# A three-layer decoder, one core: the row transposes issued ahead of the weight share's loads, and the share's thresholds and comparison moved on VectorE

## The chip, the core and the metric

The kernel runs on one core of one Trainium2 chip. The time is the device time of one execution, in microseconds (us). Before the change three runs gave 1193.79, 1201.42 and 1203.77 us, median 1201.42. The five engines each work through their own list of instructions in order, and wait for each other on semaphores: TensorE (PE) multiplies matrices, VectorE (DVE) and ScalarE (ACT) work element by element, GpSimd (POOL) does so more slowly, and SyncE (SP) issues the transfers (DMA).

## What is computed

The input `x` has 8 batches of 256 tokens and 512 features. Three residual layers follow one another:

```python
x = x + _L0_attn_ref(_layernorm(x), Wq, Wk, Wv, Wo, bo)          # 32 query heads, 8 key groups of 64, causal, tanh cap
x = x + _L0_xattn_ref(ctx_2048, ctx_2048, _layernorm(x), ssm_kernel, D, 8)
x = x + _L0_ffn_ref(_layernorm(x), w_gate_up, w_proj)
```

The feed-forward layer first rounds its weights to three values per group of 64, and this rounding is done on the chip as well:

```python
w = w_fp32.astype(bfloat16); w_g = w.reshape(-1, 64)
scale = clip(mean(abs(w_g)), 1e-8, None)
w_hat = clip(round(w_g / scale), -1, 1) * scale          # a gate_up matrix of 4096 x 512, a projection of 512 x 2048
return w + (w_hat - w)
```

## The kernel before

**Stages.** The attention of the eight batches comes first (up to about 645 us), then the convolution layer, then the feed-forward layer. Only the attention stage is touched.

**One batch of attention.** PE runs ten steps (`attend`, `STEPS = NG + 2`). In step s it does one piece of projection or output work (`filler`), the scores of head group s (`scores`), and the weighted values of group s - 2 (`values`). ACT applies tanh and exp (`soften`), POOL masks (`mask`, line 1989) and adds key halves (`add_keys`, line 1998), and DVE normalises (`normalise`). The normalised context of a group, in `ctx32`, is split in two halves of 16 bits: ACT writes the high one (`high_ctx`, line 1153), POOL the low one (`low_ctx`, line 2002), and PE's `output(b, g)` needs both.

**The tail of a batch.** Behind the ten steps PE alternates the first seven projection units of the next batch with the last three output groups: `project(b+1, 0)`, `output(b, 5)`, `project(b+1, 1)`, `output(b, 6)`, `project(b+1, 2)`, `output(b, 7)`, and then `project(b+1, 3)` to `project(b+1, 6)`. DVE turns each unit by the rotary angles (`rotate`, lines 1443 to 1446), POOL adds its parts, ACT and DVE split it (`high_unit`, `low_unit`), and SP stores it and places it again in the layout of the scores.

**The rows' turn.** The next batch's rows, standardised, are split by ACT (line 1192) and DVE (line 1625) in step 7 into `row_halves`. `turn_rows` on SP sends them through two transposing transfers into `hT_halves` (line 605). The first matmul of `project(b+1, 0)` waits for both.

**The weight share.** In each of seven batches one share of the feed-forward weights is quantised. It has 3584 columns on 128 partitions. For share b:
- SP stores the ternary weights of share b - 1 (`store_ffn`), waits until these have left, and issues the two loads of share b into `wffn` (`next_share`, lines 478 and 468, 1280 and 512 KB);
- ACT rounds them to bfloat16 in step 8 (`round_share`, line 1163), between `high_ctx(b, 5)` and `high_ctx(b, 6)`;
- DVE takes the sums and thresholds in step 9 (`find_thresholds`, lines 1562 to 1570), ahead of `normalise(b, 7)`;
- ACT spreads the thresholds over the columns into `w_cut` (`spread`, line 1167), ahead of `high_ctx(b, 7)`, and the scales behind units 1 and 2;
- DVE compares above in the tail ahead of unit 1 (`find_above`, line 1574), below in step 0 of the next batch (`find_below`, lines 1579 to 1583), and then scales the digits (`scale_digits`).

`w_cut` lies in the score buffer that group 2 uses, so ACT waits at step 2 of the next batch until `find_below` is through. SP's order around the end of a batch is `store_x2`, `late_units`, `store_ffn`, `next_share`, and in `next_inputs`: the residual's load (line 465), `turn_rows`, the load of x (line 462), and the stores and placements of the next batch's units.

## Time and profile before

| | before |
|---|---|
| runs | 1193.79, 1201.42, 1203.77 us, median 1201.42 |
| the profiled execution | 1197.75 us, its span 1196.0 us |
| PE busy | 1140.1 us (95%) |
| PE weight loads | 814.4 us (68%) |
| DVE busy | 885.7 us (74%) |
| ACT busy | 552.2 us (46%) |
| POOL busy | 679.4 us (57%) |
| mean granted clock of PE | 0.984 of full speed |

PE is busy nearly all the time, so the idle stretches of PE and the stretches in which it runs at a lower granted clock are what a change of order can win or lose. The chain that ended last is PE for the most part. A group of instructions is read as: line, engine, operation, output and inputs, and how often. Of the timeline's rows the first number is the start in us from the span's beginning, the second the duration, and brackets at the end hold the idle time ahead of the instruction and what ended it. "x2" means that the row merges two instructions.

### The profile page before, as it was taken

How to read it: one execution, taken by the hardware profiler on the slowest of the kernel's cores; microseconds unless marked ns; L12 is line 12 of the kernel's file. 1: busy time of each engine (PE TensorE's matmuls, PEld its weight loads, DVE VectorE, ACT ScalarE, POOL GpSimd, SP SyncE). 2: the span in 40 equal slices, each digit the busy share in tenths (PEclk: the TensorE clock that was granted, in tenths of full speed). 3: DMA queues.
4: the chain of work that ended last, by engine and by line, in shares of the span. 5: the costliest groups of instructions: out<-in, count | busy, mean ns of one | idle time of the engine just before them, and what ended most of it. 6: DMA issues, size and time to landing. Idle time of an engine off the chain costs nothing. (4 is left out here: it accounts for less than half of the span.)

```text
span 1196.0 us, 27031 instructions
## 1 busy us (share of the span) xinstructions
PE 1140.1 (95%) x10867; PEld 814.4 (68%) x10882; DVE 885.7 (74%) x1287; ACT 552.2 (46%) x617; POOL 679.4 (57%) x557
## 2 busy tenths in 40 slices
PE   5988998999999989999999999999999999999998
PEld 4665665756657657666576577777886876786683
DVE  6979787787788878888888588888746645754654
ACT  6866574564655645746556500000244533542441
POOL 1553492783865945947659679999343322422331
PEclk9998998998999999999999999999999999999999
DMA  9562344563454345445545457773001122013000
GB/s 325 157 227 79 120 122 119 154 170 93 150 173 141 125 120 172 141 126 155 159 140 161 170 109 142 141 142 92 1 19 23 32 54 53 8 45 53 19 19 36
DMA packets 166183, 134.15 MB, mean 112 GB/s; under 512 B 69628, under 2 KB 127362, under 8 KB 166082
## 3 DMA queue, kind: packets, MB, share of 16 engines
q1 hardware_dynamic: 141128, 126.44, 36.8%
q10 hardware_dynamic: 24960, 6.29, 3.5%
q8 instruction: 78, 1.28, 0.4%
q14 instruction: 17, 0.14, 0.0%
HBM read 81.76 MB, written 35.21 MB: 98 GB/s over the span
## 5 line engine op out<-in xcount | busy, mean ns | idle before, releaser
L701 PE MATMUL bank<-hT_halves,w_hi 128*128 128x256 f16 x640 | 179.5, 280 | 25.9 <-DMA hT_halves<-parts 20.6
L702 PE MATMUL bank<-hT_halves,w_hi 128*128 128x256 f16 x640 | 179.0, 280 | 0.0
L703 PE MATMUL bank<-hT_halves,w_lo 128*128 128x256 f16 x640 | 178.9, 280 | 0.0
L1984 POOL TENSOR_TENSOR parts<-parts 128x512 f32<-128x512 f32 x80 | 116.8, 1463 | 107.6 <-DVE parts L1446 107.6
L963 PE MATMUL bank<-kv,toep 128*128 128x288 f32 (+2 forms) x660 | 159.3, 404 | 0.7 <-ACT qT L1211 0.5
L2002 POOL TENSOR_TENSOR ctx_lo<-ctx,ctx_hi 128x512 f16<-128x512 f32 x64 | 97.7, 1526 | 89.6 <-ACT ctx_hi L1153 88.6
L963 PEld LDWEIGHTS bank<-kv,toep 128*128 128x128 f32 x660 | 124.6, 191 | 34.4 <-ACT qT L1211 0.8
L1989 POOL TENSOR_SCALAR_AFFINE_SELECT region_c<-region_c 128x512 f32<-128x512 f32 x128 | 105.5, 847 | 52.9 <-ACT region_c L1177 52.9
L2132 POOL TENSOR_TENSOR sqsum<-sqsum,toep 128x512 f32<-128x512 f32 x56 | 78.1, 1395 | 95.3 <-ACT toep L1353 95.1
L1159 ACT CAST halves<-parts 128x512 f16<-128x512 f32 x80 | 49.3, 617 | 141.4 <-POOL parts L1984 140.2
L1042 PE MATMUL bank<-odd_halves,guT 128*128 128x256 f16 x512 | 112.2, 273 | 0.0
L1041 PE MATMUL bank<-odd_halves,guT 128*128 128x256 f16 x512 | 112.2, 273 | 0.0
L1598 DVE TENSOR_TENSOR halves<-parts,halves 128x512 f16<-128x512 f32 x80 | 75.6, 944 | 49.3 <-ACT halves L1159 48.8
L1041 PE MATMUL bank<-cpair,guT 128*128 128x256 f16 x496 | 108.8, 273 | 0.3 <-DVE hid L1863 0.3
L1042 PE MATMUL bank<-cpair,guT 128*128 128x256 f16 x496 | 108.8, 273 | 0.0
L1174 ACT ACTIVATE region_c<-bank,cap_scale 128x1536 f32<-128x1536 f32 x64 | 98.1, 1532 | 20.7 <-PE bank L782 20.7
L1365 ACT ACTIVATE silu<-bank 128x512 f32<-128x512 f32 x64 | 38.0, 594 | 141.9 <-PE bank L1042 138.5
L701 PE MATMUL bank<-region_o,ctx_hi 128*128 128x512 f16 x256 | 98.3, 384 | 0.3 <-DVE parts L1446 0.2
L702 PE MATMUL bank<-region_o,ctx_hi 128*128 128x512 f16 x256 | 97.8, 382 | 0.0
L703 PE MATMUL bank<-region_o,ctx_lo 128*128 128x512 f16 x256 | 97.5, 381 | 0.0
L1177 ACT ACTIVATE region_c<-region_c 128x1536 f32<-128x1536 f32 x64 | 95.0, 1485 | 2.0
L701 PEld LDWEIGHTS bank<-hT_halves,w_hi 128*128 128x128 f16 x640 | 64.2, 100 | 44.6 <-issue 29.9
(192 smaller groups left out, 2663.2 us busy)
## 6 DMA issues: line engine op xcount, KB each, us to landing
unit_halves<-halves SPq DMA_DIRECT2D x80, 256.0 KB, 2.2
q_both<-unit_halves SPq DMA_DIRECT2D x64, 256.0 KB, 2.9
q_high<-unit_halves SPq DMA_DIRECT2D x64, 128.0 KB, 3.0
toep<-kernel_padded SPq DMA_DIRECT2D x32, 256.0 KB, 3.9
wffn<-w_gu SPq DMA_DIRECT2D x6, 1280.0 KB, 6.3
cpair<-ctx_pairs SPq DMA_DIRECT2D x32, 176.0 KB, 4.6
xin<-x SPq DMA_DIRECT2D x8, 512.0 KB, 3.9
region_o<-wq SPq DMA_DIRECT2D x4, 1024.0 KB, 11.4
```

The source lines that it names most:

```text
L701: pe.matmul(dst, lh, rh, start=first and k == 0, stop=False)
L702: pe.matmul(dst, lh, rl, start=False, stop=False)
L703: mm = pe.matmul(dst, ll, rh, start=False, stop=last and k == n - 1)
L963: mm = pe.matmul(dst, toep[:, n, d * P:(d + 1) * P], kv[:, p, m * B + batches.start:m * B + batches.stop, :], start=(m == 0), stop=(m == l))
L1041: pe.matmul(dst, guT[:, k, col:col + P], h3_hi[p][:, k, :], start=(k == 0), stop=False)
L1042: mm = pe.matmul(dst, guT[:, k, col:col + P], h3_lo[p][:, k, :], start=False, stop=(k == DB - 1))
L1174: act.activation(s.rearrange("p (n c) -> p n c", n=3), bank[:, 0:3, :], ACT.Tanh, scale=cap_scale[:, g // 2:g // 2 + 1]).then_inc(tanh_don ...
L1177: act.activation(s, s, ACT.Exp, scale=CAP).then_inc(exp_done, 1)
L1984: pool.tensor_tensor(slot[:, 0], slot[:, 0], slot[:, 1], ALU.add).then_inc(unit_summed, 1)
L1989: last = pool.affine_select(s, s, pattern=[[0, REP], [sign, P]], compare_op=ALU.is_ge, fill=0.0, base=0, channel_multiplier=-sign)
L2002: pool.tensor_tensor(ctx_lo[:, 2 * g:2 * g + 2, :], ctx32[:, g % 2], ctx_hi[:, 2 * g:2 * g + 2, :], ALU.subtract).then_inc(ctx_lo_done, 1)
L2132: pool.tensor_tensor(sqsum[:, p], sqsum[:, p], square[:, n % 2], ALU.add).then_inc(sqsum_done, 1)
```

## The change

Three things move, and no instruction is added or removed.

1. On SP, `turn_rows(b + 1)` goes from behind `next_share(b)` and `next_residual` to the place right behind `store_ffn(b - 1)`. The share's two loads and the residual's load follow it. This holds for all six batches that have a share's load at their end.
2. On DVE, `find_thresholds(b)` goes from step 9, ahead of `normalise(b, 7)`, to the tail, behind `rotate(b+1, 0)`. On ACT the spreads of the thresholds go behind units 1 and 2, and those of the scales behind units 3 and 4.
3. On DVE, `find_above` goes from the tail to step 0 of the next batch, ahead of `find_below`. The share of batch 0 has only this third part on DVE.

```diff
             def next_inputs(b):
+                turn_rows(b + 1)
+                next_share(b)
                 next_residual(b, 4 * TT * b + 2 * TT)
-                turn_rows(b + 1)
                 load_x(b + 2)
                 place_early(b + 1)
...
                 store_ffn(b - 1)
-                next_share(b)
                 next_inputs(b)
...
                 act.wait_ge(sums_filled, NG * b + LAST_IN_CUT + 1)
-                for tiles in HALVES:
-                    spread(b, gthr, w_cut, THRESHOLDS, tiles)
                 high_ctx(b, NG - 1, False)
                 for n in range(EARLY):
                     high_unit(b + 1, n)
                     if 1 <= n < 3:
-                        spread(b, gscale, w_by, THRESHOLDS, HALVES[n - 1])
+                        spread(b, gthr, w_cut, THRESHOLDS, HALVES[n - 1])
+                    if 3 <= n < 5:
+                        spread(b, gscale, w_by, THRESHOLDS, HALVES[n - 3])
...
             def attend(b):
                 for step in range(STEPS):
                     if step == 0:
+                        find_above(b - 1)
                         find_below(b - 1)
...
-                    if step == NG + 1:
-                        find_thresholds(b)
...
                 for n in range(EARLY):
-                    if n == 1:
-                        find_above(b)
                     rotate(b + 1, n)
+                    if n == 0:
+                        find_thresholds(b)
```

On SP, at the end of batch 1 (the copy ahead of the loop; the loop's copy and the last one move in the same way), the order stands as follows. `hT_halves<-parts` is the rows' turn, `wffn<-w_gu` and `wffn<-w_p` are the share's loads, `xres<-x` the residual's, `xin<-x` that of the batch after.

```order
 L487 DMA gate_up_ternary<-wffn 128x2x512
 L482 DMA proj_ternary<-wffn 128x2x256 x4
+L605 DMA_TRANSPOSE hT_halves<-parts 128x8x128 x2
 L478 DMA wffn<-w_gu 128x5x512
 L468 DMA wffn<-w_p 128x4x256
 L465 DMA xres<-x 128x2x512
-L605 DMA_TRANSPOSE hT_halves<-parts 128x8x128 x2
 L462 DMA xin<-x 128x2x512
 L527 DMA unit_halves<-halves 128x4x256 x2
```

The two transposes have moved past three loads.

On DVE, from step 9 of a batch on, before the change: the thresholds (lines 1562 to 1570), and behind them the normalisation of group 7 (lines 1455 to 1466).

```order
L1562 TENSOR_REDUCE gthr<-w_bf 128x56
L1564 ISA
L1565 TENSOR_SCALAR gscale<-gthr 128x56
L1566 REGISTER_ALU
L1567 TENSOR_SCALAR gthr<-gscale 128x56
L1568 REGISTER_ALU
L1570 TENSOR_SCALAR gthr<-gthr 128x56
L1454 REGISTER_ALU
L1455 STREAM_TRANSPOSE region_c<-bank 128x256
L1457 RECIPROCAL rinv<-region_c 128x8
L1459 STREAM_TRANSPOSE region_c<-rinv 128x256
L1466 TENSOR_TENSOR ctx<-bank,region_c 128x512
```

After the change the normalisation of group 7 stands ahead of this piece, which begins with the rotation of unit 0. Lines of the changed kernel are one lower than those of before here.

```order
L1439 ISA
L1442 TENSOR_TENSOR parts<-bank,cos_s 128x512
L1444 SCALAR_TENSOR_TENSOR parts<-bank,sin_s 128x256
L1445 TENSOR_TENSOR parts<-bank,sin_s 128x256
L1561 TENSOR_REDUCE gthr<-w_bf 128x56
L1563 ISA
L1564 TENSOR_SCALAR gscale<-gthr 128x56
L1565 REGISTER_ALU
L1566 TENSOR_SCALAR gthr<-gscale 128x56
L1567 REGISTER_ALU
L1569 TENSOR_SCALAR gthr<-gthr 128x56
```

The thresholds have moved behind one normalisation and one rotation.

On DVE, the start of the loop's body (step 0 of a batch), before the change:

```order
L1765 ISA
L1579 TENSOR_TENSOR region_c<-w_bf,region_c 128x3584
L1580 REGISTER_ALU
L1581 TENSOR_SCALAR region_c<-region_c 128x3584
L1582 REGISTER_ALU
L1583 TENSOR_TENSOR wffn<-wffn,region_c 128x3584
```

and after it, with the comparison above in front (line 1573, which was 1574):

```order
L1763 ISA
L1573 TENSOR_TENSOR wffn<-w_bf,region_c 128x3584
L1577 ISA
L1578 TENSOR_TENSOR region_c<-w_bf,region_c 128x3584
L1579 REGISTER_ALU
L1580 TENSOR_SCALAR region_c<-region_c 128x3584
L1581 REGISTER_ALU
L1582 TENSOR_TENSOR wffn<-wffn,region_c 128x3584
```

Step 0 on DVE holds one instruction over 3584 columns more.

## Rows read from the trace of the kernel before

**Rows 1.** Waits of PE: line, releaser, us in total, times, longest us.

```profile
PE bank L701 <- DMA hT_halves<-parts: 20.6, 6, 5.0
```

**Rows 2.** Timeline of PE: first matmul of project(b+1, 0), batches 1 to 4.

```profile
187.67 0.37 PE L701 MATMUL bank<-hT_halves,w_hi 128*128 128x256 f16 x1 [5.00 <-DMA hT_halves<-parts]
...
271.12 0.37 PE L701 MATMUL bank<-hT_halves,w_hi 128*128 128x256 f16 x1 [4.50 <-DMA hT_halves<-parts]
...
352.53 0.27 PE L701 MATMUL bank<-hT_halves,w_hi 128*128 128x256 f16 x1 [2.08 <-DMA hT_halves<-parts]
...
433.76 0.27 PE L701 MATMUL bank<-hT_halves,w_hi 128*128 128x256 f16 x1 [5.03 <-DMA hT_halves<-parts]
```

**Rows 3.** Timeline of SP: turns and share loads at the ends of batches 1 to 4.

```profile
179.66 4.50 SPq L605 DMA_TRANSPOSE hT_halves<-parts  x2
...
263.60 5.44 SPq L605 DMA_TRANSPOSE hT_halves<-parts  x2
...
341.55 0.39 SPq L478 DMA_DIRECT2D wffn<-w_gu  x1
...
347.43 2.97 SPq L605 DMA_TRANSPOSE hT_halves<-parts  x2
350.61 0.43 SPq L462 DMA_DIRECT2D xin<-x  x1
...
421.31 0.40 SPq L478 DMA_DIRECT2D wffn<-w_gu  x1
...
425.55 6.13 SPq L605 DMA_TRANSPOSE hT_halves<-parts  x2
```

**Rows 4.** Timeline of PE: first matmul of output(b, 6), batches 1 to 4.

```profile
197.46 0.38 PE L701 MATMUL bank<-region_o,ctx_hi 128*128 128x512 f16 x1
...
281.83 0.38 PE L701 MATMUL bank<-region_o,ctx_hi 128*128 128x512 f16 x1
...
360.35 0.38 PE L701 MATMUL bank<-region_o,ctx_hi 128*128 128x512 f16 x1
...
443.25 0.38 PE L701 MATMUL bank<-region_o,ctx_hi 128*128 128x512 f16 x1
```

**Rows 5.** Busy us (and instructions) of PE, PEld, DVE, ACT, POOL; PEclk, DMA, GB/s.

```profile
271.60:275.60 4.00, 4.00 (x21) 2.82 (x20) 3.90 (x5) 0.00 (x0) 1.16 (x1) 0.50 0.17 65
```

**Rows 6.** Timelines of ACT, POOL and DVE behind the share's load, batches 3 and 4.

```profile
349.28 3.18 ACT L1163 CAST w_bf<-wffn 128x3584 bf16<-128x3584 f32 x1 [2.45 <-DMA wffn<-w_p]
352.37 0.62 ACT L1153 ACTIVATE ctx_hi<-ctx 128x512 f16<-128x512 f32 x1
...
353.07 1.15 POOL L2002 TENSOR_TENSOR ctx_lo<-ctx,ctx_hi 128x512 f16<-128x512 f32 x1 [4.72 <-ACT ctx_hi L1153]
...
352.49 3.89 DVE L1562 TENSOR_REDUCE gthr<-w_bf 128x56 f32<-128x3584 bf16 x1 [1.80 <-ACT w_bf L1163]
...
430.50 3.18 ACT L1163 CAST w_bf<-wffn 128x3584 bf16<-128x3584 f32 x1 [5.55 <-DMA wffn<-w_p]
```

**Rows 7.** The page's DMA issues: count, KB each, median us to landing.

```profile
wffn<-w_gu SPq DMA_DIRECT2D x6, 1280.0 KB, 6.3
```

**Rows 8.** Timelines of DVE, POOL and PE: batch 2's tail, batch 3's steps 0 to 2.

```profile
278.98 2.03 DVE L1574 TENSOR_TENSOR wffn<-w_bf,region_c 128x3584 bf16<-128x3584 bf16 x1 [0.28 <-ACT region_c L1167]
...
279.56 2.46 POOL L2002 TENSOR_TENSOR ctx_lo<-ctx,ctx_hi 128x512 f16<-128x512 f32 x1 [6.75 <-ACT ctx_hi L1153]
...
304.76 2.02 DVE L1579 TENSOR_TENSOR region_c<-w_bf,region_c 128x3584 bf16<-128x3584 bf16 x1
...
307.94 2.33 DVE L1583 TENSOR_TENSOR wffn<-wffn,region_c 128x3584 bf16<-128x3584 bf16 x1
...
307.25 3.53 POOL L1989 TENSOR_SCALAR_AFFINE_SELECT region_c<-region_c 128x512 f32<-128x512 f32 x2 [3.85 <-ACT region_c L1177]
310.86 1.28 POOL L1998 TENSOR_TENSOR key_sum<-region_c 128x512 f32<-128x512 f32 x1
...
312.73 0.43 PE L814 MATMUL bank<-region_c,sum_ones 128*32 128x128 f32 x8
```

More of the change, by code:

```diff
@@ L616, in _ @@
             store_first_ffn()
-            next_share(1)
             next_inputs(1)
@@ L627, in _ @@
             store_ffn(B - 3)
+            turn_rows(B - 1)
             next_share(B - 2)
             next_residual(B - 2, 4 * TT * (B - 2) + 2 * TT)
-            turn_rows(B - 1)
             place_early(B - 1)
@@ L1655, in last_batch @@
                     if step == 0:
+                        find_above(b - 1)
                         find_below(b - 1)
@@ L1761, in first_batch @@
                 low_unit(1, EARLY - 1)
-                find_above(0)
             first_batch()
```

## The prediction, made before the changed kernel ran

> **What bounds the kernel now.** I read the page first: PE is busy 95% of the span, so what counts is where PE stands still or is slow. The list of PE's waits names one wait that comes back: the first matmul of `project(b+1, 0)` waits for the rows' turn six times, 20.6 us together [rows 1]. The timeline of PE shows four of the six: 5.00, 4.50, 2.08 and 5.03 us [rows 2]. The other two must share 20.6 - 16.61 = 3.99 us, so they are short ones like that of batch 3. So there are three long and three short waits.
>
> SP's timeline says why they differ. I call T the start of the first transpose's issue, the point at which the row halves are ready; the change leaves it alone. In batch 3 the share's load had been issued 5.9 us ahead of T (341.55 to 347.43), the two transposes took 2.97 us to issue, and PE began at T + 5.1. In batches 1, 2 and 4 they took 4.50, 5.44 and 6.13 us, and PE began at T + 8.0, 7.5 and 8.2 [rows 2, 3]; in batch 4 the load had started only 4.2 us before. The long waits are turns that queue behind a load still in flight.
>
> The long ones cost more than the wait. From `project(b+1, 0)` to `output(b, 6)` lie one output group and two projection units. That takes 7.82 us in batch 3, but 9.79, 10.71 and 9.49 us in batches 1, 2 and 4 [rows 2, 4]. Behind the idle stretch PE runs at a granted clock of 0.50, which is the 1.2 GHz level, where it had the full 2.4 GHz before [rows 5]. After the 2.08 us of batch 3 nothing of this is left over. So a long wait costs some 1.7 to 2.9 us on top.
>
> **Part 1, the turns ahead of the loads.** It gives every turn the conditions of batch 3 or better: PE can begin at T + 5.1 and reach `output(b, 6)` at T + 5.1 + 7.82 = T + 12.9. If this were all, it would be worth the sum of the offsets of `output(b, 6)` from T. These are 17.80, 18.23, 12.92 and 17.70 us now [rows 3, 4], and 12.92 for the other two: 92.5 us, against 77.5 us. That is a gain of 15.0 us.
>
> But the loads now queue behind the turns, and somebody waits for them: ACT's `round_share` stands ahead of `high_ctx(b, 6)`, and `output(b, 6)` needs that group's context. Step by step:
> - The load of x, which stood next behind the turns, was issued at T + 3.18 (347.43 to 350.61). The share's first load takes that place, after a wait for stores which left before T.
> - From its issue to ACT's start on the share took 7.73 us in batch 3 (341.55 to 349.28), giving T + 10.9.
> - The cast holds ACT for 3.09 us before `high_ctx` starts, POOL's `low_ctx` starts 0.70 us later and takes 1.15 us [rows 6]. That gives T + 15.9.
>
> PE arrives at T + 12.9 and waits 3.0 us. Before the change the load came 9 us earlier against T, and this chain was done by 354.22, 6.1 us ahead of PE's 360.35. The move uses up that cover and 3.0 us more. Six ends at T + 15.9 are 95.4 us against 92.5: **+2.9 us**. The three long ends win about 2 us each, the three short ones lose 3 us each. All later work of the tail hangs on this start, since PE runs from there to the next batch without a gap.
>
> The bounds: the longest way from load to cast is that of batch 4, 9.19 us (421.31 to 430.50), though a turn ran beside it; that adds 1.46 us to each end, 8.8 us. The shortest that a row allows is the larger load alone, 6.3 us [rows 7], which takes off 1.43 us each, 8.6 us. I take batch 3's 7.73, since there the load had the DMA engines nearly to itself, as it will behind the turns.
>
> **Part 2, the thresholds in the tail.** `find_thresholds` waits for the cast, which ends at T + 14.1. Ahead of `normalise(b, 7)` it would now hold that back too; behind `rotate(b+1, 0)` it holds back `rotate(b+1, 1)`. Its reduce takes 3.89 us [rows 6] and three short instructions follow, so it ends near T + 18.7 and the rotation near T + 20. PE needs that rotation first at `project(b+1, 4)`. At 2.6 us for each piece this begins four pieces behind `output(b, 6)`, at T + 26. The cover is 6 us, and the cost nothing. The spreads move on ACT with 2 us or more between the units. `output(b, 7)` is not late: its normalisation no longer waits. Cost: nothing.
>
> **Part 3, the comparison above in step 0.** It is one instruction of 2.03 us [rows 8]. On DVE it is covered: the rotation of unit 7 comes at most 2.03 us later, and POOL, busy masking, adds that unit's parts only well behind the first two masks. ACT's wait for `find_below` at step 2 would end at 312.3 instead of 310.3 (307.94 + 2.33), which delays the tanh of group 2 by under a microsecond; PE needs that one only behind its next projection.
>
> POOL is another matter. While DVE compares, POOL's `low_ctx` takes 2.46 us, where alone it takes 1.15 [rows 6, 8]. In step 0 POOL must mask group 0 and add its key halves for PE's sums. Before: `find_below` holds DVE from 304.76 to 310.27, the mask (two selects) takes 3.53 us, the key addition ends at 312.14, and PE takes it at 312.73, with 0.6 us to spare [rows 8]. After: with 2.03 us in front, the three instructions run to about 312.3. The mask waits for the first of them (to 308.8) and can end near 310.1, beside the second. The key addition then meets the third (310.0 to 312.3) and ends near 313.6. PE waits 0.9 us. The loop has this six times (batches 1 to 6): 6 x 0.9 = **+5.4 us**. Bounds: nothing, if POOL slips in between the instructions; or 6 x 2.1 = 12.6 us, if the mask itself waits until 312.3, ends its second select at 312.9 and the values start 1.5 us late with the key addition behind them at 314.2. The batch after the loop scales in step 1, where PE already waits for the key addition; I count nothing there.
>
> **The sum.** The profiled execution took 1197.75 us (span 1196.0). 1197.75 + 2.9 + 5.4 = **1206 us**. The median of the runs shown is 1201.42, 3.7 us more than this execution. The number of long waits is a matter of a microsecond between load and turn, so other executions will have had more of them; the change makes all ends alike, which is why I do not add the 3.7.
>
> **Rivals.**
> - **The clock falls in the new gap.** The 3.0 us ahead of `output(b, 6)` lie between 2.08 us, behind which nothing is lost, and 4.50 us, behind which 2.9 us are lost [rows 2, 4]. If it falls each time at the mean of the three losses (1.97, 2.89, 1.67: 2.2 us), that is 13 us: 1219 us; at half of the ends, 1213. Against it: 3.0 is nearer to the short wait. Chance 0.17.
> - **The load arrives early enough: faster.** This decides from one point: ACT's start on the share, 7.73 us behind the issue. If it fell to 6.3 us, the whole would be 1197.5, about no change; for the full gain it must be 4.7 us, and then 1197.75 - 15.0 + 5.4 = 1188 us. For it: the long turns really vanish. Against it: the larger of the two loads alone needs 6.3 us [rows 7]. With the POOL wait absent as well it is 1183. Chance 0.12.
> - **POOL's mask waits for all of DVE's step 0:** 1197.75 + 2.9 + 12.6 = 1213 us. For it: the mask took 3.53 us, of which about 2.3 are one DVE instruction. Against it: one of its selects ran beside the middle DVE instruction, which the change leaves in its place. Chance 0.08.
> - **The load is as slow as in batch 4:** 1206 + 8.8 = 1215 us. Chance 0.08.
>
> The Trainium skill, page "SBUF — State Buffer", section "Who interferes with whom", bears on the third rival. By it a VectorE instruction with two SBUF inputs, and a tensor_scalar in a two-port mode, hold the port pair that GpSimd reads through for the whole instruction, and the second to issue fully blocks. The trace agrees in the 2.46 us of `low_ctx`. By this rule alone the mask would also stand still beside the middle instruction, which gives the 1213 us; the 3.53 us say that one select got through, and I follow the row.
>
> **How the numbers follow.** The forecast (ends at T + 15.9, POOL between nothing and 0.9 us) has 0.55 and the range 1198 to 1212. With the rivals the range that leaves out 2 in 10 is 1190 to 1217. A measurement of this kernel tells about 1% (12 us) from no change. Faster by that is only most of the second rival: 0.10. Slower (above 1213.4): most of the clock's case, half of the last two, and a tail of the forecast: 0.20. Within 1%: 0.70.
>
> **What the profile after would show.** The waits for the rows' turn fall to six of about 2 us, 12 us together. A new wait of PE appears for POOL's `low_ctx` ahead of `output(b, 6)`, six of about 3 us, 18 us together. ACT, free near T, stands still for the share's load until T + 10.9. PE's wait for `key_sum`, 0.5 us now, grows to about 5 us. SP's transposes take 3.0 us in pairs everywhere. I am wrong if ACT starts on the share before T + 9, if PE shows no wait for the context, or if the granted clock falls behind the new gap.

## Result, and the profile after

The changed kernel takes 1226.16 us (median of four runs, 1221.73 to 1230.32), where the kernel before takes 1197.61 beside it. The ratio is 1.0263, with a 95% interval of 1.0218 to 1.0308: it is slower by 28.6 us. The forecast was 1206 us with a range up to 1217, so the time lies outside.

| | before | after |
|---|---|---|
| the profiled execution | 1197.75 us, span 1196.0 | 1230.32 us, span 1228.6 |
| PE busy | 1140.1 us (95%) | 1148.3 us (93%) |
| DVE busy | 885.7 us | 879.9 us |
| POOL busy | 679.4 us | 684.9 us |
| mean granted clock of PE | 0.984 | 0.982 |

The list of PE's waits of the kernel after, in the four lines that the change touches (line and releaser, us in total, times, longest):

```profile
PE bank L700 <- POOL ctx_lo L2000: 26.5, 6, 4.8
...
PE bank L700 <- DMA hT_halves<-parts: 8.6, 6, 1.5
PE bank L813 <- POOL key_sum L1996: 5.1, 6, 1.0
...
PE bank L700 <- DVE parts L1445: 4.6, 6, 1.6
```

The line of the rows' turn answers to [rows 1]: 20.6 us of waiting have become 8.6. The context's wait was not there before, and the other two stood at 0.5 and 0.2 us:

```profile
PE bank L814 <- POOL key_sum L1998: 0.5, 1, 0.5
PE bank L701 <- DVE parts L1446: 0.2, 1, 0.2
```

The three lines now hold 36.2 us, and the turn gives back 12.0. PE is also busy 8.2 us longer, though its work is the same.

One end of a batch shows how it goes. Here are SP, ACT, POOL and PE at the end of batch 2, where T is 268.51 (start, duration, instruction, idle time ahead of it):

```profile
268.51 2.79 SPq L605 DMA_TRANSPOSE hT_halves<-parts  x2
271.59 0.41 SPq L478 DMA_DIRECT2D wffn<-w_gu  x1
...
272.94 0.27 PE L700 MATMUL bank<-hT_halves,w_hi 128*128 128x256 f16 x1 [1.44 <-DMA hT_halves<-parts]
...
280.39 3.18 ACT L1162 CAST w_bf<-wffn 128x3584 bf16<-128x3584 f32 x1 [12.48 <-DMA wffn<-w_p]
283.48 1.14 ACT L1152 ACTIVATE ctx_hi<-ctx 128x512 f16<-128x512 f32 x2
...
284.18 2.26 POOL L2000 TENSOR_TENSOR ctx_lo<-ctx,ctx_hi 128x512 f16<-128x512 f32 x2 [14.76 <-ACT ctx_hi L1152]
...
285.39 0.59 PE L700 MATMUL bank<-region_o,ctx_hi 128*128 128x512 f16 x1 [4.46 <-POOL ctx_lo L2000]
...
289.68 0.27 PE L700 MATMUL bank<-hT_halves,w_hi 128*128 128x256 f16 x1
```

The turn is quick now, and PE is at `project(b+1, 0)` at T + 4.4, where [rows 2, 3] had T + 7.5 for this batch. But ACT then stands still for 12.48 us until the share has arrived, and the high half of group 6's context waits behind it. PE reaches `output(b, 6)` and idles 4.46 us. The wait is not all of it. `output(b, 6)` then takes 4.29 us to the next unit (285.39 to 289.68), where the same twelve matmuls take 2.60 at the full clock. The windows of that stretch show why (busy us and instructions of PE, PEld, DVE, ACT, POOL, then PEclk, DMA share, GB/s):

```profile
281.39:285.39 4.00, 0.00 (x1) 0.01 (x1) 1.79 (x1) 3.23 (x3) 1.21 (x2) 1.00 0.06 22
285.39:287.39 2.00, 2.00 (x5) 0.71 (x6) 2.00 (x1) 0.00 (x0) 2.00 (x2) 0.51 0.00 0
287.39:289.39 2.00, 2.00 (x7) 0.80 (x6) 1.90 (x7) 0.62 (x1) 0.27 (x1) 0.63 0.00 0
289.39:291.39 2.00, 2.00 (x19) 1.64 (x17) 0.70 (x2) 0.14 (x1) 1.64 (x1) 1.00 0.18 54
```

PE does nothing in the first window. In the second its granted clock is 0.51, the level of 1.2 GHz, and 5 matmuls of 512 columns fall into 2 us; at the full level it is 10 of the same matmuls (the run with the filled gap, below). The 19 of the last window have half the columns each. So the idle 4.46 us cost 1.7 us more.

All six ends, worked out from the timeline's rows in the same way (us; "to the values" is what the stretch from `output(b, 6)` to the first matmul of the next batch's value projection, `bank<-w_hi,hT_halves`, took; it is 18.28 us in all six ends of before):

```
                          b=1    b=2    b=3    b=4    b=5    b=6    sum
T                       181.30 268.51 353.97 439.94 524.98 610.66
output(b, 6) at T +      16.66  16.88  17.26  16.10  17.05  17.01  101.0
idle ahead of it          4.32   4.46   4.83   3.69   4.63   4.61   26.5
to the values            21.02  19.98  19.74  19.98  19.67  21.20  121.6
load issued to cast       8.91   8.80   9.18   8.03   8.97   9.18
```

The account of the 32.6 us between the two profiled executions (1228.6 and 1196.0) is this: 8.5 us from the later starts of `output(b, 6)` (101.0 against 92.5 before), 11.9 us lost at the low clock behind the idle stretch (121.6 less six times 18.28), 4.6 us from the wait for the key halves (5.1 against 0.5), and 4.4 us from the wait for DVE's rotation (4.6 against 0.2). These are 29.4 us. About 1.6 more lie ahead of the first T; 1.6 are not placed.

### The profile page after: what moved, and what is told of

Read it like the earlier page. It is cut to its first block and busy times, and to the rows that moved or that the text cites. A ratio compares the mean times of both kernels' runs of the same rounds, so it can differ in the third digit from the quotient of the medians.

```text
span 1228.6 us, 27043 instructions
## 1 busy us (share of the span) xinstructions
PE 1148.3 (93%) x10867; PEld 813.7 (66%) x10882; DVE 879.9 (72%) x1287; ACT 551.1 (45%) x617; POOL 684.9 (56%) x557
## 3 DMA queue, kind: packets, MB, share of 16 engines
q8 instruction: 78, 1.28, 0.4%
## 5 line engine op out<-in xcount | busy, mean ns | idle before, releaser
L700 PE MATMUL bank<-hT_halves,w_hi 128*128 128x256 f16 x640 | 177.2, 277 | 13.7 <-DMA hT_halves<-parts 8.6
L1982 POOL TENSOR_TENSOR parts<-parts 128x512 f32<-128x512 f32 x80 | 121.0, 1514 | 120.9 <-DVE parts L1445 120.9
L701 PE MATMUL bank<-hT_halves,w_hi 128*128 128x256 f16 x640 | 176.8, 276 | 0.0
L2000 POOL TENSOR_TENSOR ctx_lo<-ctx,ctx_hi 128x512 f16<-128x512 f32 x64 | 89.1, 1396 | 102.4 <-ACT ctx_hi L1152 101.6
L700 PE MATMUL bank<-region_o,ctx_hi 128*128 128x512 f16 x256 | 102.7, 401 | 31.1 <-POOL ctx_lo L2000 26.5
L1996 POOL TENSOR_TENSOR key_sum<-region_c 128x512 f32<-128x512 f32 x56 | 100.0, 1785 | 4.7
L701 PE MATMUL bank<-region_o,ctx_hi 128*128 128x512 f16 x256 | 102.1, 399 | 0.0
L702 PE MATMUL bank<-region_o,ctx_lo 128*128 128x512 f16 x256 | 101.5, 396 | 0.0
L1597 DVE TENSOR_TENSOR halves<-parts,halves 128x512 f16<-128x512 f32 x80 | 67.8, 848 | 42.1 <-ACT halves L1158 41.7
## 6 DMA issues: line engine op xcount, KB each, us to landing
region_o<-wq SPq DMA_DIRECT2D x4, 1024.0 KB, 11.7
```

The costliest lines, as they stand in the source:

```text
L700: pe.matmul(dst, lh, rh, start=first and k == 0, stop=False)
L701: pe.matmul(dst, lh, rl, start=False, stop=False)
L702: mm = pe.matmul(dst, ll, rh, start=False, stop=last and k == n - 1)
L1982: pool.tensor_tensor(slot[:, 0], slot[:, 0], slot[:, 1], ALU.add).then_inc(unit_summed, 1)
L1996: pool.tensor_tensor(key_sum[:, g % 2], sc_first[:, g % 3, :, P:S], sc_second[:, g % 3], ALU.add).then_inc(keys_added, 1)
L2000: pool.tensor_tensor(ctx_lo[:, 2 * g:2 * g + 2, :], ctx32[:, g % 2], ctx_hi[:, 2 * g:2 * g + 2, :], ALU.subtract).then_inc(ctx_lo_done, 1)
```

## Experiments

Theory A is that account: part 1 makes PE wait for the share's load through ACT, the clock then falls, and part 3 makes PE wait for POOL and DVE in the next batch. The rivals were that one of the three parts does it alone, that the slower load comes from a transfer behind it, and that the low clock is not caused by the idle stretch. Each run is compared with runs of the kernel before on the same chip; those had medians of 1196.9 to 1199.7 us. A ratio below is the time divided by theirs, with its 95% interval.

### Each part alone

**Part 1 alone**, on the kernel before:

```diff
             def next_inputs(b):
+                turn_rows(b + 1)
+                next_share(b)
                 next_residual(b, 4 * TT * b + 2 * TT)
-                turn_rows(b + 1)
                 load_x(b + 2)
...
                 store_ffn(b - 1)
-                next_share(b)
                 next_inputs(b)
```

> Part 1 of the change alone: the turns ahead of the share's loads on SP, all else as before. Theory A (the loads, now behind the turns, reach ACT's cast late, the cast stands ahead of high_ctx(b, 6), PE waits for that group's context and then runs at the lower clock): as slow as in the changed kernel ahead of output(b, 6), so 8.5 us for the later starts and 12 us for the clock: about 1218 us, and up to 3 us more, since the thresholds now hold normalise(b, 7) back: 1216 to 1223. Theory B (parts 2 and 3 on VectorE cost the time, the turns are harmless): 1183 to 1198 us.

Measured: 1238.81 us, ratio 1.0372 (1.0305 to 1.0439). This is slower than all three parts together, and well above the 1216 to 1223 us expected. Its waits of PE:

```profile
PE bank L700 <- POOL ctx_lo L2001: 39.5, 12, 4.8
```

PE waits for a context twelve times now, not six. The second of each pair stands at the other group:

```profile
284.46 0.61 PE L700 MATMUL bank<-region_o,ctx_hi 128*128 128x512 f16 x1 [4.46 <-POOL ctx_lo L2001]
...
293.67 0.39 PE L700 MATMUL bank<-region_o,ctx_hi 128*128 128x512 f16 x1 [1.00 <-POOL ctx_lo L2001]
```

With the thresholds still in step 9, DVE holds `normalise(b, 7)` until the late share has been reduced, and ACT holds `high_ctx(b, 7)` behind the spreads. The ends of the batches account for it: 8.2 us from the later starts of `output(b, 6)`, 14.7 us from the second wait, and 18.4 us lost between there and the next batch's values, mostly at the low clock behind the two stretches. That is 41.3 us, where the profiled executions lie 40.5 us apart. So part 1 alone loses the most, and part 2 wins beside it: part 1 alone is 39.9 us over its kernel before, all three parts 28.6, and the latter contain part 3.

**Parts 2 and 3 without part 1** (SP's order is that of before):

```diff
             def next_inputs(b):
-                turn_rows(b + 1)
-                next_share(b)
                 next_residual(b, 4 * TT * b + 2 * TT)
+                turn_rows(b + 1)
...
                 store_ffn(b - 1)
+                next_share(b)
                 next_inputs(b)
```

> Parts 2 and 3 alone: the changed kernel with SP's order of before. Theory A: the waits of PE for the context ahead of output(b, 6) are gone; what stays is the comparison above in step 0, seen after the change as 5.1 us of waits for key_sum and 4.6 us for the rotation ahead of output(b, 0): 1198 + 9 = 1207 us (1203 to 1210). Theory B: nearly all of the loss, 1218 us or more.

**Part 3 alone**, on the kernel before:

```diff
                     if step == 0:
+                        find_above(b - 1)
                         find_below(b - 1)
...
                 for n in range(EARLY):
-                    if n == 1:
-                        find_above(b)
                     rotate(b + 1, n)
```

> Part 3 of the change alone: the kernel before with the comparison above moved to step 0. Parts 2 and 3 together gave 1.0129 of the time before. If the comparison in step 0 is all of that: waits for key_sum 5.5 us, for the rotation ahead of output(b, 0) 4.7 us, 1.008 to 1.013, that is 1208 to 1213 us. If the thresholds' place in the tail shares in it: key_sum waits alone, 1203 us.

Measured: parts 2 and 3 take 1211.70 us, ratio 1.0129 (1.0058 to 1.0199); part 3 alone takes 1210.00 us, ratio 1.0104 (1.0062 to 1.0146). These two lines of PE's waits are the same, figure for figure, in both:

```profile
PE bank L814 <- POOL key_sum L1997: 5.5, 6, 1.0
PE bank L701 <- DVE parts L1446: 4.7, 6, 1.6
```

The two kernels have the same new waits of the same size, and their times can't be told apart. So part 2 by itself costs nothing that these runs can show, and part 3 costs about 12 us alone. The two waits grew by 9.5 us against before. In the profiled execution of parts 2 and 3, 3.7 us more are lost between T and the next values, at the low clock. There the wait for the turn at the end of batch 3 is 2.08 us, just as in [rows 2], but the clock fell behind it:

```profile
350.69 0.27 PE L701 MATMUL bank<-hT_halves,w_hi 128*128 128x256 f16 x1 [2.08 <-DMA hT_halves<-parts]
...
360.19 0.38 PE L701 MATMUL bank<-region_o,ctx_hi 128*128 128x512 f16 x1
```

From the one row to the other it takes 9.50 us, where it was 7.82 before. (The profiled execution of part 3 alone is the slowest of its five, 1218.00 us, with 24.7 us of waiting for the turn.)

### Part 3: where DVE is late

**The comparison above back in the tail**, at another place than before, between the low halves of units 5 and 6; the rest as after:

```diff
                     if step == 0:
-                        find_above(b - 1)
                         find_below(b - 1)
...
                             output(b, i)
+                find_above(b)
                 low_unit(b + 1, EARLY - 1)
```

> The changed kernel with the comparison above taken out of step 0 and put into the tail, between the low halves of units 5 and 6, where VectorE waits for ScalarE. If the comparison in step 0 makes both new waits (key_sum and the rotation of unit 9), 9 us go: 1217 us. If only the key_sum wait is its doing: 1221 us. If it is harmless: 1226 us.

Measured: 1222.73 us, ratio 1.0232 (1.0158 to 1.0306). Waits of PE, and POOL's key addition of step 0 in one batch:

```profile
PE bank L778 <- DMA q_high<-unit_halves: 5.3, 4, 1.9
PE bank L700 <- DVE parts L1445: 4.7, 6, 1.6
```

```profile
398.41 2.96 POOL L1996 TENSOR_TENSOR key_sum<-region_c 128x512 f32<-128x512 f32 x1
```

The time can't be told from that of the kernel after (ratio 1.0263), so the waits must decide. The wait for the key halves is gone from the list, so that one belongs to the comparison in step 0. The wait for the rotation stays as it was. Here the comparison took 3.09 us instead of 2.03, and the comparison below began 5.68 us behind the first matmul of the value projection, where it was 4.65 us before and 6.32 us after. POOL's key addition still ran beside DVE, for 2.96 us instead of 1.28, and ended 12.67 us behind that matmul, against 12.03 before and 13.29 after: early enough for PE's sums, but POOL stays 0.6 us late for what follows. That is the size of the wait for the rotation in five of the six batches (the section on the prediction follows it). PE's waits for the placed units grew as well, to 5.3 us from 2.3 after.

### Part 1: what makes the share late

**x's load behind the placements of the units:**

```diff
                 next_residual(b, 4 * TT * b + 2 * TT)
-                load_x(b + 2)
                 place_early(b + 1)
+                load_x(b + 2)
```

> The changed kernel with the load of x, which follows the share's loads, put behind the stores and placements of the next batch's units. After the change the way from the share's first load to the cast takes 8.85 us on average, where I had counted 7.73. Theory C (the loads that follow at once, the residual's and that of x, take bandwidth from the share's): with one of the two gone the way shrinks to about 8.0, output(b, 6) starts 0.8 us sooner, 1226 - 5 = 1221 us. Rival (the turns in front hold the share's loads up): the way stays 8.85 and the time 1226 us.

Measured: 1227.06 us, ratio 1.0238 (1.0190 to 1.0286). From the load's issue to ACT's start on it lie 8.85, 8.74, 8.98, 8.19, 9.26 and 7.77 us, mean 8.63 against 8.85 after. The load of x is not what slows the share.

**SP waits until the turned rows have landed**, and only then issues the share's loads:

```diff
                 turn_rows(b + 1)
+                sp.wait_ge(hT_in, 16 * TT * b)
                 next_share(b)
```

> The changed kernel, but SP waits until both transposes have landed before it issues the share's loads, which puts them some 1.3 us later (T + 4.4 in place of T + 3.1). If the transposes still in flight are what stretches the way from load to cast (8.85 us instead of 7.73), the way shrinks to 7.6 to 7.8 and the cast starts where it did, T + 12.0. If not (the loads' own pace, or the residual's load behind them), the way stays 8.8 and the cast starts at T + 13.2.

Measured: 1233.93 us, one run. From issue to cast it now takes 8.50, 7.53, 8.05, 7.86, 9.00 and 8.61 us, mean 8.26 against 8.85. That fits the transposes in flight having about 0.6 us in it, but it does not show it. In the kernel before, the six ends took 7.71, 8.86, 7.73, 9.19, 7.73 and 7.54 us, so the 7.73 us of batch 3 is one of the short ones of a wide spread. And in the run with the digits early (below) the load of batch 3 took 9.02 us, although the turn was issued only behind the cast's start:

```profile
338.62 0.39 SPq L478 DMA_DIRECT2D wffn<-w_gu  x1
...
347.64 3.18 ACT L1163 CAST w_bf<-wffn 128x3584 bf16<-128x3584 f32 x1 [0.38 <-DMA wffn<-w_p]
...
347.85 2.81 SPq L605 DMA_TRANSPOSE hT_halves<-parts  x2
```

So a load is as slow as after the change with no transpose beside it, and what makes it so stays open. The wait costs more than it brings: the cast starts at T + 12.7 in the mean, where it was T + 11.8, and PE's waits for the context grow:

```profile
PE bank L702 <- POOL ctx_lo L2002: 31.8, 6, 6.1
```

### The clock behind the idle stretch

**The idle stretch filled:** 36 matmuls of 256 columns behind `project(b+1, 1)`, into a bank whose content nobody reads. They are extra work: six times 36 makes 216 more, 11098 matmuls instead of 10882.

```diff
                     project(b + 1, n)
+                    if n == 1:
+                        for k in range(36):
+                            pe.matmul(bank[:, unit_bank(2), 0:S], w_hi[:, k % DB, 0:P], hT_hi[:, k % DB, :], start=True, stop=True)
```

> The changed kernel with 36 further matmuls of 256 columns (3.9 us at full clock, results unused) behind project(b+1, 1), where PE stands still for 3.7 to 4.8 us. If the slow stretch behind the gap comes from the idle time, the clock stays at full speed there and output(b, 6) takes 2.6 us instead of 4.0 to 5.1: 11.7 us less, 1226 - 12 = 1214 us, though PE does more work. If the slow output(b, 6) has another cause (the group's operands, contention), it stays at 4 to 5 us: 1226 us or more.

Measured: 1223.01 us, ratio 1.0221 (1.0161 to 1.0281); the profiled execution has a span of 1221.1 us and a clock of 0.990. PE at the end of batch 2 and the window behind it:

```profile
285.36 0.39 PE L700 MATMUL bank<-region_o,ctx_hi 128*128 128x512 f16 x1 [0.82 <-POOL ctx_lo L2003]
...
287.96 0.27 PE L700 MATMUL bank<-hT_halves,w_hi 128*128 128x256 f16 x1
```

```profile
285.39:287.39 2.00, 2.00 (x10) 0.94 (x11) 2.00 (x1) 0.00 (x0) 2.00 (x2) 1.00 0.00 0
```

The matmul starts at the same time as after (285.36 and 285.39), since the share is as late as before. But the granted clock is 1.00 where it was 0.51, and the twelve matmuls take 2.60 us, in all six ends. That shows the low clock to be a consequence of the idle stretch, and not of the work around it. From T to the values the six ends take 213.8 us in sum, against 222.6 after: 8.8 less. The forecast was 12; one turn was long in this execution (a wait of 3.44 us and a low clock behind that) and took back most of the rest. The medians alone would not have shown it: they lie 3 us below the kernel after, and 4 below the run with x's load behind, which was on the same chip and has five of the six gaps, with intervals of 6 to 7 us to each side.

### The share off the path

**The cast behind the last context:** `round_share` behind `high_ctx(b, 7)`.

```diff
-                    if step == NG:
-                        round_share(b)
-                act.wait_ge(sums_filled, NG * b + LAST_IN_CUT + 1)
                 high_ctx(b, NG - 1, False)
+                round_share(b)
+                act.wait_ge(sums_filled, NG * b + LAST_IN_CUT + 1)
```

> The changed kernel with ScalarE's rounding of the share moved behind high_ctx(b, 7), so that no context waits for the load. Theory A: PE reaches output(b, 6) at T + 12.2 without a gap; the 26.5 us of waits for ctx_lo and the 12 us of lower clock go: 1226 - 38 = 1188 us. The thresholds then end near T + 20 and the rotation of unit 1 near T + 21.5, just ahead of PE's need at T + 22.7. Rival (what costs is the traffic of turns and loads itself, or thresholds behind the rotation): no better than 1220 us.

Measured: 1210.20 us, ratio 1.0123 (1.0058 to 1.0188), clock 0.994. Waits of PE:

```profile
PE bank L778 <- DVE parts L1444: 8.6, 6, 1.6
PE bank L700 <- DVE parts L1444: 8.2, 10, 1.6
PE bank L813 <- POOL key_sum L1995: 6.2, 6, 1.0
...
PE bank L700 <- ACT v_s L1120: 4.0, 6, 0.8
```

The waits for the context are gone and with them the low clock: this is 16 us less than after, and the edit is only where ACT takes the share. That settles that ACT's order, and not the load itself, puts the share on PE's path. The expected 1188 us did not come: these four lines hold 27.0 us, where the kernel after has 10.1 in the same ones. The thresholds, which DVE takes behind unit 0, wait for the later cast and hold back the units' chain.

**The whole share later:** the cast behind `high_unit(b+1, 0)`, the thresholds behind `low_unit(b+1, 0)`, the comparison above at the end of the tail, the scales behind units 4 and 5.

```diff
                     high_unit(b + 1, n)
+                    if n == 0:
+                        round_share(b)
+                        act.wait_ge(sums_filled, NG * b + LAST_IN_CUT + 1)
                     if 1 <= n < 3:
                         spread(b, gthr, w_cut, THRESHOLDS, HALVES[n - 1])
-                    if 3 <= n < 5:
-                        spread(b, gscale, w_by, THRESHOLDS, HALVES[n - 3])
+                    if 4 <= n < 6:
+                        spread(b, gscale, w_by, THRESHOLDS, HALVES[n - 4])
...
                     rotate(b + 1, n)
-                    if n == 0:
-                        find_thresholds(b)
                     if n:
                         low_unit(b + 1, n - 1)
+                    if n == 1:
+                        find_thresholds(b)
...
                             output(b, i)
+                find_above(b)
                 low_unit(b + 1, EARLY - 1)
```

> A kernel that keeps the turns ahead of the loads and takes everyone out of the load's way: ScalarE rounds the share behind the high half of unit 0, VectorE takes the thresholds behind the low half of unit 0 (the rotation of unit 1 no longer waits), the scales are spread behind units 4 and 5, the comparison above stands ahead of the last low half of the tail. By theory A the waits for ctx_lo and the lower clock go, by the waits seen with the cast late (rotations ahead of scores 0, 8.6 us; ahead of output(b, 0); key_sum) most of the new ones too. Each tail then takes the 31.2 us of the short-wait batches before: 1198 - 15 = 1183 us, plus up to 8 us where step 0 on VectorE is late: 1183 to 1192. Rival (VectorE's tail is too full for the comparison): about as slow as before, 1198 us or more.

The same with the scales one unit sooner, behind units 3 and 4:

```diff
-                    if 4 <= n < 6:
-                        spread(b, gscale, w_by, THRESHOLDS, HALVES[n - 4])
+                    if 3 <= n < 5:
+                        spread(b, gscale, w_by, THRESHOLDS, HALVES[n - 3])
```

> The kernel with the share taken late (1190.8 us), with the scales spread behind units 3 and 4 instead of 4 and 5. There PE waited at the batch's start 3.4 us for v_s and 1.7 us for the tanh, six and four times, since ScalarE came late out of the tail. If the spreads behind unit 5 are the reason, 3 to 4 us go: 1187 us. Otherwise 1191 us.

Measured: 1190.81 us (nine runs), ratio 0.9953 (0.9927 to 0.9979), and 1189.64 us (ten runs), ratio 0.9939 (0.9909 to 0.9969). Both are faster than the kernel before, by about half a per cent, and than the kernel after by 3%. They can't be told from each other. Waits of PE of the first:

```profile
PE bank L700 <- DMA hT_halves<-parts: 11.3, 6, 2.9
...
PE bank L700 <- DVE parts L1445: 4.4, 6, 1.6
...
PE bank L700 <- ACT v_s L1120: 3.4, 6, 0.8
```

Here the turn's move does what the forecast said it would do if nobody waited for the load: no wait for the context, shorter turns. In four ends the time from T to the values is 30.5 us. In the other two it is 33.7: the wait for the turn was just under 3 us there, and the clock fell behind it:

```profile
186.33 0.27 PE L700 MATMUL bank<-hT_halves,w_hi 128*128 128x256 f16 x1 [2.92 <-DMA hT_halves<-parts]
...
190.17 0.63 PE L700 MATMUL bank<-region_o,ctx_hi 128*128 128x512 f16 x1
```

That unit took 3.84 us instead of 2.62. The wait for the rotation is still there, as with the comparison at the end of the tail above.

### The turns' price by itself

**The late share with the turns behind the loads:** ACT's and DVE's order of the version with the scales behind units 4 and 5, with SP's order of the kernel before.

```diff
             def next_inputs(b):
-                turn_rows(b + 1)
-                next_share(b)
                 next_residual(b, 4 * TT * b + 2 * TT)
+                turn_rows(b + 1)
...
                 store_ffn(b - 1)
+                next_share(b)
                 next_inputs(b)
```

> The same kernel with the share taken late, but with SP's order of before (turns behind the loads): what the turns' move is worth once nobody waits for the load. If the turns ahead are worth the long waits and the clock behind them, this kernel is slower than 1190.8 by about 10 us: 1201 us (about 1.003 of the time before, with the comparison in the tail costing a little). If the gain of that kernel came from the late share alone: 1191 us or less.

Measured: 1206.29 us (ten runs), ratio 1.0047 (1.0017 to 1.0076), and 21.5 us of waiting for the turn. The version with the turns ahead (scales one unit sooner, which made no difference above) took 1189.64 on the same chip: 17 us less by the medians and 13 by the ratios, somewhat more than the 10 expected. So part 1 is worth about what the forecast's first step gave it, 15.0 us, as soon as nobody waits for the load. SP's rows of a long turn (this execution is the slowest of the ten):

```profile
424.98 0.39 SPq L478 DMA_DIRECT2D wffn<-w_gu  x1
...
429.18 6.14 SPq L605 DMA_TRANSPOSE hT_halves<-parts  x2
```

At 5.90 us behind the load the pair is issued in 3.05 us, at 4.20 us in 6.14. The six ends:

```
load to turn, us    6.47   5.19   5.90   4.20   5.90   4.41
pair's issue, us    3.33   4.99   3.05   6.14   3.16   4.91
PE's wait, us       2.41   4.06   2.17   5.21   2.27   5.39
```

The turn is long where it comes 5.2 us or less behind the load.

**The turn's distance changed from the other side:** on the kernel before, the last digits step of DVE, which the stores and so the load wait for, moved from step 5 to step 4.

```diff
-                    if 4 <= step < 6:
-                        scale_digits(b - 1, step - 3)
+                    if step == 4:
+                        scale_digits(b - 1, 1)
+                        scale_digits(b - 1, 2)
```

> The kernel before, with the last step of the digits taken from step 5 to step 4, straight behind the one ahead of it. The ternary weights are stored, and the next share's loads issued, about 2.5 us sooner against the turn. If a turn is long only when it is issued less than some 5 us behind the load, all six waits for the rows' turn are then near 2 us (12 us in all instead of 20.6) and the lower clock behind them goes too: up to 15 us less, 1183 to 1190 us. Rival (the length of a turn does not hang on that distance): waits stay 20 us and the time 1197; or the normalisation held back by 2.4 us costs PE waits, 1200 us.

Measured: 1200.93 us (ten runs), ratio 1.0020 (0.9989 to 1.0051). Waits of PE:

```profile
PE bank L701 <- DMA hT_halves<-parts: 13.8, 6, 3.6
...
PE bank L814 <- DVE region_c L1455: 6.6, 12, 0.9
```

The loads now go out 9.2 to 9.8 us ahead of the turn. Four turns cost a wait of 1.82 us and two still 3.56 and 2.95, so the distance is not all that makes a turn long. The six ends are 11.7 us shorter in sum, and the steps give that back: those that took in the digits hold up `normalise`, 6.6 us of waiting. The rest of what is given back is not placed. The expected 1183 to 1190 us did not come; the time is what the last rival had given, 1200 us.

## Why the prediction was wrong

**The rows' turn: right.** The waits fell to six short ones, 8.6 us in sum where the forecast had 12, with PE at T + 4.4 instead of T + 5.1. The pair's issue took 2.7 to 2.8 us.

**"That gives T + 15.9": the mechanism right, a term mis-sized.** The new wait came where it was forecast, six times, and ACT stood still for the share. But "from its issue to ACT's start on the share took 7.73 us" was one reading, batch 3 of before; the six ends of before take 7.54 to 9.19 us, 8.13 in the mean. In the changed kernel it takes 8.85 us, so that `output(b, 6)` starts at T + 16.8 in the mean: +8.5 us instead of +2.9, most of the way to the upper bound that batch 4's 9.19 us had given.

**"3.0 is nearer to the short wait": the step that failed.** By it the sum put nothing for the clock. The idle stretch became 4.4 us: the context came 0.9 us later than forecast, and PE, through the quicker turn, 0.5 us sooner, at T + 12.4. That is as long as the 4.50 us behind which [rows 2, 4] had already shown a loss. The clock fell in all six ends and took 11.9 us; the rival that had a chance of 0.17 had priced it at 13. The step would have been unsafe at 3.0 us as well. Its short end was a single reading: behind the same 2.08 us the clock fell in the execution of parts 2 and 3, and over all kept executions it fell behind six of ten stretches of 2.8 to 3.3 us. The stretch itself came out longer for one reason. The forecast let PE's arrival get earlier only as a gain, while the length of the idle stretch is the difference of two times, and each error in either goes into it in full.

**Part 2, no cost: right.** Parts 2 and 3 together show the waits of part 3 alone. What the forecast missed is its worth: part 1 without parts 2 and 3 takes 1238.81 us.

**"PE waits 0.9 us" for the key addition: right.** 5.1 us against 5.4. POOL's row of the changed kernel, beside DVE's third instruction:

```profile
315.19 2.33 DVE L1582 TENSOR_TENSOR wffn<-wffn,region_c 128x3584 bf16<-128x3584 bf16 x1
...
312.49 3.16 POOL L1987 TENSOR_SCALAR_AFFINE_SELECT region_c<-region_c 128x512 f32<-128x512 f32 x2 [4.22 <-ACT region_c L1176]
315.73 2.93 POOL L1996 TENSOR_TENSOR key_sum<-region_c 128x512 f32<-128x512 f32 x1
...
318.71 0.43 PE L813 MATMUL bank<-region_c,sum_ones 128*32 128x128 f32 x8 [0.52 <-POOL key_sum L1996]
```

The addition took 2.93 us where [rows 8] had 1.28. The Trainium skill, page "SBUF — State Buffer", section "Who interferes with whom", has the second to issue blocked while VectorE holds the port, and the 2.93 us fit that. So does the mask. Its two selects end at 314.21 and 315.65, each 0.5 us behind the end of a DVE instruction (313.71 and 315.16); one select gets in between two instructions. The forecast's row showed that, and its reading that the rule would hold the mask until 312.9 went too far: the rule does not exclude the gap between two instructions.

**"On DVE it is covered": right, but POOL's delay was followed only to its first consumer.** A new wait for DVE's rotation stands six times in the list, 4.6 us:

```profile
332.48 0.39 PE L700 MATMUL bank<-region_o,ctx_hi 128*128 128x512 f16 x1 [0.61 <-DVE parts L1445]
```

DVE's own delay is not the reason. The rotation of unit 7 ended at 318.79, and POOL came to its parts at 322.94 only. POOL is the engine without slack here. From the first mask on it stands still for 0.17 us in all until these parts, while ACT and DVE behind it do stand still:

```profile
318.62 3.00 POOL L1987 TENSOR_SCALAR_AFFINE_SELECT region_c<-region_c 128x512 f32<-128x512 f32 x2
...
322.94 1.27 POOL L1982 TENSOR_TENSOR parts<-parts 128x512 f32<-128x512 f32 x1
...
324.33 0.62 ACT L1158 CAST halves<-parts 128x512 f16<-128x512 f32 x1 [3.64 <-POOL parts L1982]
...
324.98 0.94 DVE L1597 TENSOR_TENSOR halves<-parts,halves 128x512 f16<-128x512 f32 x1 [1.89 <-ACT halves L1158]
```

Before, POOL took unit 7's parts here:

```profile
316.43 1.28 POOL L1984 TENSOR_TENSOR parts<-parts 128x512 f32<-128x512 f32 x1
```

Measured from the first matmul of the value projection (300.11 before, 305.37 after), the mask begins at 7.1 us in both, the key addition ends at 12.03 and 13.29, the parts begin at 16.32 and 17.57, and DVE's low half of unit 7 begins at 18.37 and 19.62. So the 1.25 us that POOL lost beside DVE go on through ACT and DVE to the rotations of units 8 and 9. In part 1 alone, where the comparison stays in the tail, the addition took 1.28 us in five of the six batches, and the wait for the rotation is 0.5 us in all. In five batches the wait is 0.6 us. In the last one it is 1.58 us; there DVE also scales the digits in step 1, and the runs don't separate the two.

The sum of the forecast's steps with the measured sizes is 8.5 + 11.9 + 4.6 + 4.4 = 29.4 us, against the 8.3 that it gave.

## What to carry over

Before a transfer is moved back in a queue, look for the instruction that waits for it and for what stands behind that one on its engine: here one cast held the context of a group for which the whole tail waited. Moving the cast alone turned +2.6% into +1.2%, and with the thresholds, the comparison and the scales moved too it became -0.5 to -0.6%. The length of a new idle stretch on TensorE is a difference of two arrivals; price it with both at their bounds, and add what the clock takes behind it, 1.4 to 2.9 us each here. A delay of an engine without slack, here POOL, is not over at its first consumer: follow it through that engine's next instructions until the engine stands still.

## What the runs showed of the hardware

- **Idle time and clock.** The 14 kept traces have about 110 idle stretches of TensorE of more than 1.2 us ahead of `project(b+1, 0)` or `output(b, 6)`. Up to 1.9 us none was followed by the lower clock. From 2.0 to 2.4 us it was 6 of 10, from 2.8 to 3.9 us 10 of 17, and from 4.06 us on all 35. In the ends worked out above each fall cost 1.4 to 2.9 us. So two stretches of the same length can end differently, as the 2.08 us of batch 3 did in the kernel before and with parts 2 and 3. In the run with x's load behind, 3.85 us cost nothing:

```profile
456.59 0.39 PE L700 MATMUL bank<-region_o,ctx_hi 128*128 128x512 f16 x1 [3.85 <-POOL ctx_lo L2000]
...
459.19 0.27 PE L700 MATMUL bank<-hT_halves,w_hi 128*128 128x256 f16 x1
```

  The unit behind it took 2.60 us. Between 2.0 and 3.9 us the length alone doesn't decide; what else does stays open.
- **Transposing transfers behind a load.** In the changed kernel, with the load behind it, a pair is issued in 2.7 to 2.8 us. In the four executions with the turns behind the loads (before, parts 2 and 3, part 3 alone, the late share) it took 4.4 to 6.2 us where a load of 1792 KB had been issued 4.2 to 5.2 us before it by the same engine, and 2.7 to 3.3 us where it was 5.7 us or more. Other things can make a pair long as well: in the last end of the late share it took 4.40 us with the turns ahead.
- **The load from issue to use.** It takes 7.5 to 9.3 us where the cast waits for it, in either order. The means of six ends are 8.1 to 8.3 us with the turns behind it (before, parts 2 and 3, part 3 alone) and 8.6 to 8.85 us with the turns ahead of it. In the run in which SP waits for the turns to land it is 8.26 us. What makes a single end long is not settled.
